# Other instruction orders at the end of a memory stage and in the last stage of a four-layer kernel

## The chip, the cores and the metric

The kernel runs on one core of one Trainium2 chip. The metric is the device time of one execution in microseconds (us), the median of three runs.

## The reference

Four blocks follow one another on 4096 tokens of width 256, each with a residual and a layer normalization: gated linear attention, a mixture of experts, a neural memory, and an MLP with ternary weights. The change touches the end of the third and all of the fourth. Cut to what matters:

```python
# third block (memory): a two-layer residual MLP (W1, W2) is trained for one step on all tokens
keys, queries, values = x @ Wk + bk, x @ Wq + bq, x @ Wv + bv
grads = grad of sum(mean((lmm(params, keys) - values)**2) * alr)
params = p * (1 - LR * WD) - LR * g / (sqrt(g * g) + EPS)
x = layernorm(x + lmm(new_params, queries))      # h = h + silu(h @ W + b), twice
# fourth block
h = relu(x @ Wq1.T + b1)                          # Wq1, Wq2: weights rounded to -1, 0, 1
x = layernorm(x + h @ Wq2.T + b2)
```

## The kernel before

The tokens are cut into eight blocks of 512 (`NB = 8`), called tiles here. X holds the tokens by rows, XT by columns. Each engine has its own hand-written list of instructions, and semaphores order them among the engines; nothing is planned at run time, so an instruction that waits holds up everything behind it on its engine. A product of a 512-token tile with a 256x256 weight (`plane`, line 1230) writes a pair of PSUM banks and shows as 8 matmul records.

**The memory stage** (`build_memory`, line 1238) makes the gradients. PSUM has a ring of three bank pairs there, and `pair(q, use)` picks a pair from the tile's number and one of 11 uses in fixed rotation; two more banks collect the gradients of W1 and W2. For the last tile, q = 7, TensorE (PE) does the second layer, `grad1` of tile 6, the turns of h0 and h1 (transposes that ScalarE, ACT, copies out), then `back` (W2T times dz2), the turn of dz2, `grad2`, the turn of dz1 and `grad1`. Among these stand five products `queries(0)` to `queries(4)` (query projections of tiles 0 to 4, which the next stage needs; ACT evicts each with its bias into XT, line 1582). VectorE (DVE) makes dz2 (line 1718) and dz1 (1732), and at the end the optimizer step of W2 after `g2_ready` and of W1 after `g1_ready` (lines 1803 to 1807). The stage ends when all engines have ended their lists.

**The last stage** (`build_read_and_mlp`, line 1833) reads the memory with the new weights and applies the MLP. An iteration q handles three tiles at once: of tile q `first` (banks RA), `second` (banks RB) and `turn_h`; of tile q - 1 `normalize` on ACT (line 2100) and `turn_x`, `x_hi`, `x_lo`; of tile t = q - 2 the MLP: eight `up(t, f)` (line 1948, 4 matmul records, one bank each, `bH[f % 2]`), ACT's two evictions `hidden(t, f)` (lines 2094 and 2095), the subtraction on GpSimd (POOL, line 2298) and eight `down(t, f)` (line 1958, 8 records, sums over f in the banks bO). `up(t, f)` waits until ACT has read its bank for f - 2; `down(t, f)` waits for POOL's `hl_done`. `down(t, 6)` and `down(t, 7)` slip into the next iteration, ahead of its `up`s. After the last `down`, DVE adds the result (`add_out`, line 2195); `down(t, 0)` waits for the `add_out` of tile t - 1 (`out_done`). `finish(q - 4, ..)` on ACT (line 2107) is the last normalization of a tile, from scales that DVE computes (`scales`, lines 2314 to 2320 and 2236). Iteration q = 2 has its own list on PE, `third`; the last two tiles are done by `drain`, with four banks for `up`; DVE ends with `last_half(0)` and `last_half(1)` (lines 2246 to 2263).

DVE's order in a middle iteration is: `first` (lines 2162 and 2171, the h1 add), `add_out`, its statistics, `add_b2` (2201), `x_lo` (2207), `second`, the residual, statistics, `scales`.

Of the kernel before, what the change touches and what calls it, by code (L numbers as in the profile page):

```python
# [1226 lines left out]
NB = NTOK // 512  # L1227
# [10 lines left out]
def build_memory(nc, io, mem):  # L1238

    X, XT, ident, slot = mem["X"], mem["XT"], mem["ident"], mem["slot"]  # L1240
    with ExitStack() as c2:
# [52 lines left out]
        td2_ready, td2_read, td1_ready, td1_read = sem("td2_ready"), sem("td2_read"), sem("td1_ready"), sem("td1_read")  # L1294
# [13 lines left out]
        def pair(q, use):  # L1308

            return ring[(11 * q + use) % 3]  # L1310

        with nc.Block() as block:
            @block.sync
            def _(sp):
# [26 lines left out]
            def _(pe):  # L1341
# [45 lines left out]
                def back(q):  # L1387
                    if q + 1 < NB:
                        pe.wait_ge(k_read, 2 * (q + 2))
                    else:  # L1390
                        pe.wait_ge(q_read, 2)
                    pe.wait_ge(dz2_done, 2 * (q + 1))
                    plane(pe, pair(q, DH), W2T, lambda i: dz2[:, i, :]).then_inc(dh_ready, 1)

# [10 lines left out]
                def turn_h1(q):  # L1405
                    pe.wait_ge(sl2_done, 2 * (q + 1))
                    turn(pair(q, TH1), h1).then_inc(th1_ready, 1)

                def turn_dz2(q):
                    if q + 1 < NB:  # L1410
                        pe.wait_ge(v_read, 2 * (q + 2))
                    else:
                        pe.wait_ge(q_read, 4)
                    turn(pair(q, TD2), dz2).then_inc(td2_ready, 1)

                def turn_dz1(q):
                    pe.wait_ge(dz1_done, 2 * (q + 1))
                    turn(pair(q, TD1), dz1).then_inc(td1_ready, 1)
# [8 lines left out]
                def grad1(q):  # L1427
                    pe.wait_ge(th0_read, 2 * (q + 1))
                    pe.wait_ge(td1_read, 2 * (q + 1))
                    grad(0, "h0", "dz1").then_inc(g1_ready, 1)  # L1430
# [6 lines left out]
                def queries(j, b):  # L1437
                    plane(pe, b, Wq, tokens(j)).then_inc(q_ready, 1)
# [8 lines left out]
                q = NB - 1  # L1447
# [44 lines left out]
                grad1(q - 1)  # L1492
                turn_h0(q)
                turn_h1(q)
                pe.wait_ge(th0_read, 2 * NB)
                queries(0, pair(q, KEY))
                pe.wait_ge(td1_read, 2 * (NB - 1))
                queries(1, pair(q, VAL))
                back(q)
                turn_dz2(q)  # L1500
                pe.wait_ge(th1_read, 2 * NB)
                queries(2, pair(q, Z1))
                grad2(q)
                pe.wait_ge(dh_done, 2 * (q + 1))
                turn_dz1(q)
                grad1(q)
                pe.wait_ge(td2_read, 2 * NB)
                queries(3, pair(q + 1, Z2))
                pe.wait_ge(q_read, 2 * 3)
                queries(4, pair(q + 1, TH0))  # L1510

            @block.scalar
            def _(act):
# [65 lines left out]
                def queries(j, b):  # L1579
                    act.wait_ge(q_ready, j + 1)  # L1580
                    for g in range(G):
                        act.activation(XT[:, g, j * 512:(j + 1) * 512], b[g][:, :], ACT.Identity, bias=bq[:, g:g + 1]).then_inc(q_read, 1)
# [35 lines left out]
                second(q)  # L1618
                keep_h0(q)
                keep_h1(q)  # L1620
                queries(0, pair(q, KEY))
                queries(1, pair(q, VAL))
                keep_dz2(q)
                queries(2, pair(q, Z1))
                keep_dz1(q)
                queries(3, pair(q + 1, Z2))
                queries(4, pair(q + 1, TH0))

            @block.vector
            def _(v):  # L1630
# [202 lines left out]
def build_read_and_mlp(nc, io, mem, out):  # L1833
# [4 lines left out]
    with ExitStack() as c2:  # L1838
# [31 lines left out]
        def block_of(q):  # L1870
            return 0 <= q < NB
# [4 lines left out]
        with nc.Block() as block:  # L1876
# [18 lines left out]
            def _(pe):  # L1895
# [7 lines left out]
                def second(q):  # L1903
                    if q >= 1:
                        pe.wait_ge(res_done, 2 * q)
                    pe.wait_ge(h1_done, 2 * (q + 1))
                    plane(pe, RB, W2n, lambda i: h1[:, i, :]).then_inc(z2_ready, 1)
# [44 lines left out]
                def down(q, f):  # L1952
                    pe.wait_ge(hl_done, FC * q + f + 1)
                    if f == 0 and q >= 1:
                        pe.wait_ge(out_done, 2 * q)
                    for k in range(4):
                        for part in range(2):
                            mm = pe.matmul(bO[k // 2][:, (k % 2) * D:(k % 2 + 1) * D], hr[:, part, f, k * P:(k + 1) * P], W2r[:, f, :],  # L1958
                                           start=(f == 0 and part == 0 and k % 2 == 0), stop=(f == FC - 1 and part == 1), skip_group_check=True)
                        if f == FC - 1 and k % 2 == 1:  # L1960
                            mm.then_inc(o_ready, 1)
# [13 lines left out]
                def third():  # L1975
                    first(2)
                    turn_h(1)
                    for f in range(4):
                        up(0, f)
                    down(0, 0)  # L1980
                    second(2)
                    down(0, 1)
                    turn_x(1)
                    down(0, 2)
                    up(0, 4)
                    down(0, 3)
                    up(0, 5)
                    turn_h(2)
                    down(0, 4)
                    up(0, 6)  # L1990
                    down(0, 5)
                    up(0, 7)
# [28 lines left out]
                for q in range(NB):  # L2021
                    t = q - 2
                    if q == 2:
                        third()
                        continue
                    if block_of(q):
                        first(q)
                    if q == 0:
                        queries(5, bH)
                    if q == 1:  # L2030
                        pe.wait_ge(q_read, 2)
                        queries(7, bH)
                    if block_of(q - 3):
                        down(q - 3, 6)
                        down(q - 3, 7)
                    if block_of(t):
                        up(t, 0)
                        up(t, 1)
                        up(t, 2)
                        up(t, 3)  # L2040
                        down(t, 0)
                        down(t, 1)
                    if block_of(q - 1):
                        turn_x(q - 1)
                    if block_of(q):
                        second(q)
                    if q == 0:
                        queries(6, bO)
                    if block_of(t):
                        down(t, 2)  # L2050
                        up(t, 4)
                        down(t, 3)
                        up(t, 5)
                    if q != 1:
                        turn_h(q)
                    if block_of(t):
                        down(t, 4)
                        up(t, 6)
                        down(t, 5)
                        up(t, 7)  # L2060
# [3 lines left out]
            def _(act):  # L2064
# [52 lines left out]
                for q in range(NB + 3):  # L2117
                    t = q - 2
                    if block_of(q):
                        first(q)  # L2120
                    if q == 0:
                        act.wait_ge(wq_in, 32)
                        queries(5, 0, bH)
                    if block_of(q - 4):
                        finish(q - 4, 0, 2)
                    if block_of(t):
                        if t == 0:
                            act.wait_ge(b_in, 32)
                        hidden(t, 0)
                        hidden(t, 1)  # L2130
                    if block_of(q - 1) and q != 2:
                        normalize(q - 1)
                    if q == 1:
                        queries(7, 2, bH)
                    if block_of(t):
                        hidden(t, 2)
                        hidden(t, 3)
                    if q == 2:
                        normalize(1)
                        second(2)  # L2140
                    if block_of(q - 1):
                        x_hi(q - 1)
                    if block_of(q) and q != 2:
                        second(q)
                    if q == 0:
                        queries(6, 1, bO)
                    if block_of(t):
                        for f in range(4, FC):
                            hidden(t, f)
                    if block_of(q - 4):  # L2150
                        finish(q - 4, 2, 4)
# [276 lines left out]
```

## Time and profile before

| | us |
|---|---|
| median of three runs | 1381.18 |
| lowest and highest | 1378.48 and 1381.18 |
| the profiled execution | 1380.95 |
| its span (first to last instruction) | 1379.2 |
| PE busy in the span | 1312.8 (95%) |
| DVE, ACT, POOL busy | 803.0, 573.7, 300.9 |

The profiled execution is one run with the hardware profiler; its time is its span and 1.75 us around it. In a timeline a row is a run of like instructions: start, length, engine, line, operation, what is written from what, count, and in brackets how long the engine was idle before and what released it. Two lengths may overlap, since an instruction starts before the one ahead has fully drained; the distance between starts is the pace.

### The profile page before, as it was taken

The numbers are of one execution on the slowest core, as the hardware profiler recorded it, in microseconds if no ns is written. First come the engines' busy times: TensorE is split into PE (matmuls) and PEld (weight loads), VectorE is DVE, ScalarE is ACT, GpSimd is POOL, SyncE is SP. The second block draws the span as 40 slices with busy tenths as digits, with TensorE's granted clock in tenths as the row PEclk, the third lists the DMA queues.
The fourth block names the chain that finished last, engine by engine and source line by source line (L and its number), as shares of the span: only waits on it lengthen the run. The fifth ranks groups of instructions, "written<-read, shape, count | busy, mean of one in ns | idle before, by whom it ended". The sixth has DMA issues, their size and how long they took to land. (4 is left out here: it accounts for less than half of the span.)

```text
span 1379.2 us, 22623 instructions
## 1 busy us (share of the span) xinstructions
PE 1312.8 (95%) x7786; PEld 831.0 (60%) x7788; DVE 803.0 (58%) x1558; ACT 573.7 (42%) x1256; POOL 300.9 (22%) x345
## 2 busy tenths in 40 slices
PE   8899999899998999999999999889999999999997
PEld 4556666645555666666666665446665564577776
DVE  6999999965541222222222222477778755776777
ACT  5667777551110222222222221334343532566676
POOL 1133333314760000000000000732220000234444
PEclk9999999999999999999999999999999999999999
DMA  7666665666220111111111111423110000000001
GB/s 233 213 211 215 213 209 192 219 227 215 93 97 15 39 46 46 46 46 46 43 45 43 44 46 42 142 66 103 39 39 8 8 8 12 1 1 16 16 31 62
DMA packets 78342, 118.47 MB, mean 86 GB/s; under 512 B 9489, under 2 KB 63025, under 8 KB 74289
## 3 DMA queue, kind: packets, MB, share of 16 engines
q1 hardware_dynamic: 71696, 100.52, 22.1%
q0 software_dynamic: 6144, 16.79, 3.8%
q8 instruction: 53, 0.87, 0.3%
q14 instruction: 33, 0.26, 0.1%
q10 hardware_dynamic: 416, 0.03, 0.0%
HBM read 84.98 MB, written 32.33 MB: 85 GB/s over the span
## 5 line engine op out<-in xcount | busy, mean ns | idle before, releaser
L1824 POOL DMA_INDIRECT m_got<-outs,slot x64 | 62.7, 980 | 543.1 <-DMA outs<-XT 450.6
L1209 DVE TENSOR_TENSOR ro_h<-ro_bB,ro_sl 128x512 f32<-128x512 f32 x71 | 49.1, 692 | 217.2 <-PE ro_bB L1158 217.2
L2298 POOL TENSOR_TENSOR q_hr<-q_hf,q_hr 128x512 fp32r<-128x512 f32 x64 | 84.0, 1324 | 264.8 <-ACT q_hr L2095 264.8
L625 DVE TENSOR_TENSOR_SCAN a_dcy<-a_gbc,a_ident 128x2048 f32<-128x2048 f32 x31 | 137.7, 4443 | 3.9
L1165 PEld LDWEIGHTS ro_bO<-Wout,ro_hT 128*128 128x128 f32 x568 | 107.9, 190 | 45.6 <-issue 34.6
L1153 PE MATMUL ro_bA<-Win,ro_xT 128*128 x284 | 134.6, 596 | 0.7 <-ACT ro_xT L1180 0.6
L1165 PE MATMUL ro_bO<-Wout,ro_hT 128*128 x568 | 134.3, 379 | 0.9 <-DVE ro_hT L1202 0.9
L1158 PE MATMUL ro_bB<-Wsw,ro_xT 128*128 x284 | 133.5, 592 | 0.0
L1189 ACT ACTIVATE XT<-ro_bO 128x256 f32<-128x256 f32 x71 | 27.2, 383 | 204.9 <-PE ro_bO L1165 204.9
L1202 DVE COPY ro_hT<-ro_bH 128x512 f32<-128x512 f32 x71 | 49.1, 692 | 101.2 <-PE ro_bH L1138 101.2
L1158 PEld LDWEIGHTS ro_bB<-Wsw,ro_xT 128*128 128x128 f32 x284 | 54.0, 190 | 67.9 <-issue 67.9
L1184 ACT ACTIVATE ro_sl<-ro_bA 128x512 f32<-128x512 f32 x71 | 42.4, 597 | 96.0 <-PE ro_bA L1153 96.0
L1054 POOL DMA_INDIRECT rows<-r_row,r_rix x64 | 63.6, 994 | 53.7 <-DVE r_rix L955 35.8
L642 DVE TENSOR_TENSOR a_A<-a_bS,a_dcy 128x1024 f32<-128x1024 f32 x64 | 75.1, 1215 | 0.1
L721 POOL TENSOR_TENSOR a_qk<-a_eb,a_rb 128x512 f32<-128x512 f32 x28 | 36.6, 1308 | 160.7 <-ACT a_eb L470 160.7
L1153 PEld LDWEIGHTS ro_bA<-Win,ro_xT 128*128 128x128 f32 x284 | 48.3, 190 | 35.5 <-issue 35.1
L1958 PE MATMUL q_bO<-W2r,q_hr 128*128 128x256 f32 x448 | 66.2, 294 | 1.4 <-POOL q_hr L2298 1.4
L1958 PEld LDWEIGHTS q_bO<-W2r,q_hr 128*128 128x128 f32 x448 | 58.0, 188 | 12.1 <-POOL q_hr L2298 6.5
L1234 PE MATMUL m_ring<-m_h,m_W 128*128 128x512 f32 x128 | 60.6, 618 | 4.6 <-DVE m_h L1674 3.5
L1948 PE MATMUL q_bH<-q_xr,W1r 128*128 128x512 f32 x224 | 61.3, 402 | 2.6 <-ACT q_hr L2095 2.6
L906 ACT ACTIVATE sh_sl<-sh_bA 128x512 f32<-128x512 f32 x28 | 16.7, 596 | 112.1 <-PE sh_bA L836 104.5
L1423 PE MATMUL m_gW<-m_t_dz,m_t_h 128*128 128x256 f32 x256 | 57.9, 379 | 1.3 <-ACT m_t_dz L1561 1.3
(302 smaller groups left out, 2484.4 us busy)
## 6 DMA issues: line engine op xcount, KB each, us to landing
a_gbc<-gd SPq DMA_DIRECT2D x31, 1024.0 KB, 5.1
rows<-a_zero SPq DMA_DIRECT2D x8, 1152.0 KB, 9.4
XT<-rows SPq DMA_DIRECT2D x71, 128.0 KB, 2.0
outs<-XT SPq DMA_DIRECT2D x71, 128.0 KB, 1.7
a_xt<-in_xTt SPq DMA_DIRECT2D x8, 512.0 KB, 5.8
X<-in_x SPq DMA_DIRECT2D x8, 512.0 KB, 4.0
Win<-in_w_in SPq DMA_DIRECT2D x8, 512.0 KB, 10.3
Wsw<-in_w_sw SPq DMA_DIRECT2D x8, 512.0 KB, 10.1
```

What stands on the lines that cost most here:

```text
L625: v.tensor_tensor_scan(dcy[:, :], gbc[j % 2][:, :], ident16[:, :], 0.0, ALU.mult, ALU.add).then_inc(d_done, 1)
L642: v.tensor_tensor(A[j % 2][:, 2 * h:2 * h + 2, :, :, :].rearrange("p r g e t -> p r g (e t)"), bS[:, 2 * h:2 * h + 2, :].rearrange("p r (g ...
L1054: pool.indirect_dma_start(out=mem["rows"], out_offset=bass.IndirectOffsetOnAxis(ap=rix[p][k][:, 0:1], axis=0), in_=row[p][k][:, :], in_off ...
L1153: mm = pe.matmul(bA[:, :], xT[p][:, g, :], w, start=(g == 0), stop=(g == G - 1))
L1158: mm = pe.matmul(bB[:, :], xT[p][:, g, :], w, start=(g == 0), stop=(g == G - 1))
L1165: mm = pe.matmul(bO[:, 0:D], hT[:, j * P:(j + 1) * P], Wout[:, bass.ds(e, 1), j, :].rearrange("p o f -> p (o f)"), start=(j == 0), stop=(j ...
L1234: mm = pe.matmul(banks[o][:, :], W[:, i, col + o * P:col + (o + 1) * P], rhs(i), start=(i == 0), stop=(i == G - 1))
L1423: mm = pe.matmul(gW[k][:, i * D:(i + 1) * D], tok[left][:, t, i * P:(i + 1) * P], tok[right][:, t, :], start=False, stop=False, skip_group ...
L1824: pool.indirect_dma_start(out=got[q % 2][k][:, t, :], out_offset=None, in_=mem["outs"], in_offset=bass.IndirectOffsetOnAxis(ap=slot[:, k, ...
L1948: mm = pe.matmul(hidden_bank(q, f)[:, :], W1r[:, g, f * P:(f + 1) * P], xr[q % 2][:, part, g, :], start=(g == 0 and part == 0), stop=(g == ...
L1958: mm = pe.matmul(bO[k // 2][:, (k % 2) * D:(k % 2 + 1) * D], hr[:, part, f, k * P:(k + 1) * P], W2r[:, f, :], start=(f == 0 and part == 0 ...
L2298: pool.tensor_tensor(hr[:, 1, f, :], hf[f % 2][:, :], hr[:, 0, f, :], ALU.subtract).then_inc(hl_done, 1)
```

## The change

Four edits of order; no instruction is added or removed, and no arithmetic changes.

- Memory stage, PE and ACT: the five query products stand at other places and use other bank pairs. `queries(0)` takes the pair VAL and no longer waits for `th0_read`; `back` follows it and no longer waits for a query eviction; `queries(2)` stands between the turn of dz1 and `grad1`.
- Last stage, PE, `third`: `down(0, 1)` goes ahead of `second(2)`.
- Last stage, PE, iterations 3 to 7: `down(t - 1, 6)` and `down(t - 1, 7)` go behind `up(t, 0)` and `up(t, 1)`, as `drain` already has it for tile 6.
- Last stage, ACT, iterations 8 to 10: `finish(q - 4, 0, 2)` goes behind `hidden(t, 0)` and `hidden(t, 1)`.

```diff
--- before.py
+++ after.py
@@ -1309,6 +1309,8 @@
 
             return ring[(11 * q + use) % 3]
 
+        last_bank = [pair(NB - 1, use) for use in (VAL, TH1, TD2, Z1, TD1)]
+
         with nc.Block() as block:
             @block.sync
             def _(sp):
@@ -1387,8 +1389,6 @@
                 def back(q):
                     if q + 1 < NB:
                         pe.wait_ge(k_read, 2 * (q + 2))
-                    else:
-                        pe.wait_ge(q_read, 2)
                     pe.wait_ge(dz2_done, 2 * (q + 1))
                     plane(pe, pair(q, DH), W2T, lambda i: dz2[:, i, :]).then_inc(dh_ready, 1)
 
@@ -1410,7 +1410,7 @@
                     if q + 1 < NB:
                         pe.wait_ge(v_read, 2 * (q + 2))
                     else:
-                        pe.wait_ge(q_read, 4)
+                        pe.wait_ge(q_read, 2)
                     turn(pair(q, TD2), dz2).then_inc(td2_ready, 1)
 
                 def turn_dz1(q):
@@ -1492,22 +1492,23 @@
                 grad1(q - 1)
                 turn_h0(q)
                 turn_h1(q)
+                pe.wait_ge(td1_read, 2 * (NB - 1))
+                queries(0, last_bank[0])
                 pe.wait_ge(th0_read, 2 * NB)
-                queries(0, pair(q, KEY))
-                pe.wait_ge(td1_read, 2 * (NB - 1))
-                queries(1, pair(q, VAL))
                 back(q)
                 turn_dz2(q)
                 pe.wait_ge(th1_read, 2 * NB)
-                queries(2, pair(q, Z1))
+                queries(1, last_bank[1])
                 grad2(q)
                 pe.wait_ge(dh_done, 2 * (q + 1))
                 turn_dz1(q)
+                pe.wait_ge(td2_read, 2 * NB)
+                queries(2, last_bank[2])
                 grad1(q)
-                pe.wait_ge(td2_read, 2 * NB)
-                queries(3, pair(q + 1, Z2))
-                pe.wait_ge(q_read, 2 * 3)
-                queries(4, pair(q + 1, TH0))
+                pe.wait_ge(q_read, 2 * 2)
+                queries(3, last_bank[3])
+                pe.wait_ge(td1_read, 2 * NB)
+                queries(4, last_bank[4])
 
             @block.scalar
             def _(act):
@@ -1618,13 +1619,12 @@
                 second(q)
                 keep_h0(q)
                 keep_h1(q)
-                queries(0, pair(q, KEY))
-                queries(1, pair(q, VAL))
+                queries(0, last_bank[0])
                 keep_dz2(q)
-                queries(2, pair(q, Z1))
+                queries(1, last_bank[1])
                 keep_dz1(q)
-                queries(3, pair(q + 1, Z2))
-                queries(4, pair(q + 1, TH0))
+                for j in range(2, 5):
+                    queries(j, last_bank[j])
 
             @block.vector
             def _(v):
@@ -1978,8 +1978,8 @@
                     for f in range(4):
                         up(0, f)
                     down(0, 0)
+                    down(0, 1)
                     second(2)
-                    down(0, 1)
                     turn_x(1)
                     down(0, 2)
                     up(0, 4)
@@ -2030,12 +2030,11 @@
                     if q == 1:
                         pe.wait_ge(q_read, 2)
                         queries(7, bH)
-                    if block_of(q - 3):
-                        down(q - 3, 6)
-                        down(q - 3, 7)
                     if block_of(t):
                         up(t, 0)
+                        down(t - 1, 6)
                         up(t, 1)
+                        down(t - 1, 7)
                         up(t, 2)
                         up(t, 3)
                         down(t, 0)
@@ -2121,13 +2120,15 @@
                     if q == 0:
                         act.wait_ge(wq_in, 32)
                         queries(5, 0, bH)
-                    if block_of(q - 4):
+                    if block_of(q - 4) and q < NB:
                         finish(q - 4, 0, 2)
                     if block_of(t):
                         if t == 0:
                             act.wait_ge(b_in, 32)
                         hidden(t, 0)
                         hidden(t, 1)
+                    if q >= NB:
+                        finish(q - 4, 0, 2)
                     if block_of(q - 1) and q != 2:
                         normalize(q - 1)
                     if q == 1:
```

## Rows read from the trace of the kernel before

**Rows 1.** The page's busy time, share of the span and instructions of each engine

```profile
PE 1312.8 (95%) x7786; PEld 831.0 (60%) x7788; DVE 803.0 (58%) x1558; ACT 573.7 (42%) x1256; POOL 300.9 (22%) x345
```

**Rows 2.** Timeline, PE, end of the memory stage (start us, us, what, idle before, releaser)

```profile
1119.47 1.91 PE L1398 MATMUL m_ring<-ident,m_h 128*128 128x128 f32 x16
1121.68 7.13 PE L1234 MATMUL m_ring<-XT,m_Wq 128*128 128x512 f32 x16 [0.30 <-ACT m_t_h L1561]
...
1132.96 3.60 PE L1234 MATMUL m_ring<-XT,m_Wq 128*128 128x512 f32 x8
...
1139.85 1.04 PE L1398 MATMUL m_ring<-ident,m_dz 128*128 128x128 f32 x8
1142.15 3.69 PE L1423 MATMUL m_gW<-m_t_dz,m_t_h 128*128 128x256 f32 x16 [1.27 <-ACT m_t_dz L1561]
1145.68 7.03 PE L1234 MATMUL m_ring<-XT,m_Wq 128*128 128x512 f32 x16
1154.32 3.67 PE L1234 MATMUL q_RA<-XT,W1n 128*128 128x512 f32 x8 [1.61 <-PEq L1312]
```

**Rows 3.** Timeline, DVE, end of the memory stage

```profile
1124.35 0.09 DVE L1718 DVE_READ_ACCUMULATOR2_ANT m_btmp<- 128x1 f32 x1
...
1140.12 0.69 DVE L1803 TENSOR_SCALAR m_ga<-m_gW 128x512 f32<-128x512 f32 x1 [4.12 <-PE m_gW L1423]
...
1151.96 0.69 DVE L1807 SCALAR_TENSOR_TENSOR W1n<-m_W,m_ga 128x512 f32<-128x512 f32 x1
```

**Rows 4.** Timeline, PE, then ACT, third tile of the last stage (q = 2)

```profile
1193.13 3.67 PE L1234 MATMUL q_RB<-q_h,W2n 128*128 128x512 f32 x8 [1.65 <-DVE q_h L2171]
...
1197.59 1.52 PE L1930 MATMUL q_RA<-ident,X 128*128 128x128 f32 x8
...
1196.54 2.08 ACT L2100 ACTIVATE X<-X,q_shift,q_rstd 128x256 f32<-128x256 f32 x4 [4.43 <-DVE q_shift L2236]
```

**Rows 5.** Timeline, PE, one middle tile (q = 4)

```profile
1235.47 2.46 PE L1958 MATMUL q_bO<-W2r,q_hr 128*128 128x256 f32 x16
1237.77 2.03 PE L1948 MATMUL q_bH<-q_xr,W1r 128*128 128x512 f32 x8
1240.22 2.36 PE L1948 MATMUL q_bH<-q_xr,W1r 128*128 128x512 f32 x8 [0.42 <-ACT q_hr L2095]
1242.42 2.06 PE L1958 MATMUL q_bO<-W2r,q_hr 128*128 128x256 f32 x16
```

**Rows 6.** Timeline, ACT, then DVE, the same tile

```profile
1237.23 1.08 ACT L2107 ACTIVATE X<-X,q_shift,q_rstd 128x256 f32<-128x256 f32 x2
1238.91 0.69 ACT L2094 ACTIVATE q_hf<-q_bH,q_b 128x512 f32<-128x512 f32 x1 [0.59 <-PE q_bH L1948]
...
1238.20 1.28 DVE L2171 TENSOR_TENSOR q_h<-XT,q_sl 128x512 f32<-128x512 f32 x2
1239.40 1.28 DVE L2195 TENSOR_TENSOR X<-q_bO,X 128x512 f32<-128x512 f32 x2
...
1246.10 1.29 DVE L2207 TENSOR_TENSOR q_xr<-q_RA,q_xr 128x512 fp32r<-128x512 f32 x2 [2.22 <-ACT q_xr L2087]
```

**Rows 7.** Timeline, DVE in tile q = 2, then POOL in tile q = 3

```profile
1189.79 3.19 DVE L2171 TENSOR_TENSOR q_h<-XT,q_sl 128x512 f32<-128x512 f32 x2
...
1215.39 2.54 POOL L2298 TENSOR_TENSOR q_hr<-q_hf,q_hr 128x512 fp32r<-128x512 f32 x2 [4.97 <-ACT q_hr L2095]
```

**Rows 8.** Timeline, PE, then ACT, first part of the drain

```profile
1339.14 1.21 PE L1958 MATMUL q_bO<-W2r,q_hr 128*128 128x256 f32 x8 [1.39 <-POOL q_hr L2298]
1340.18 1.17 PE L1930 MATMUL q_RA<-ident,X 128*128 128x128 f32 x8
...
1335.50 1.10 ACT L2107 ACTIVATE X<-X,q_shift,q_rstd 128x256 f32<-128x256 f32 x2 [1.25 <-DVE q_shift L2236]
...
1338.78 2.08 ACT L2100 ACTIVATE X<-X,q_shift,q_rstd 128x256 f32<-128x256 f32 x4
```

**Rows 9.** Timeline, DVE, the last half tile

```profile
1371.61 0.69 DVE L2246 TENSOR_TENSOR X<-q_bO,X 128x512 f32<-128x512 f32 x1 [0.17 <-PE q_bO L1970]
```

## The prediction

> **What bounds the kernel now.** I read the page first: PE is busy 95% of the span, no other engine over 58% [rows 1]. So time can only come from PE's idle gaps, and an order that leaves a gap where it was gains nothing. Then I took PE's timeline through the stretches that the diff touches and read the brackets: how long PE waited, and for whom. At the memory stage's end it waits 0.30 us for the turned h0, 1.27 us for the turned dz1, and 1.61 us for ACT's last eviction and the change of stage [rows 2]. In the third tile of the last stage it waits 1.65 us for DVE's h1 add [rows 4]. Each of the five middle tiles (q = 3 to 7) has the same gap at its third `up`, 0.42 us by the bracket [rows 5]. In the drain it waits 1.39 us for POOL [rows 8]. For each gap the other engines' timelines say what would be late next.
>
> **Memory stage.** Same work, other order, so I lay it out anew from 1119.47. Paces come from starts: 16 transposes 1.74 (8 are 0.87), a product 3.43, a gradient 3.46; the last two sum to 1139.85 - 1132.96 = 6.89 [rows 2]. `queries(0)` no longer waits: 1121.21 instead of 1121.68. It ends at 1124.64; dz2 is ready at 1124.44 [rows 3], so `back` follows at once, to 1128.07. Turn of dz2 to 1128.94, `queries(1)` to 1132.37, `grad2` to 1135.83, turn of dz1 to 1136.70, `queries(2)` to 1140.13, `grad1` to 1143.59. The 1.27 us wait for ACT's copy of dz1 is covered by `queries(2)`, three times as long. `queries(3)` and `(4)` start at 1143.59 instead of 1145.68 [rows 2], a gain of 2.09. The remaining waits (ACT's evictions of about 1.3 us) each lie behind a product of 3.43. Is DVE late next? Its two optimizer steps take 12.53 us from `grad2`'s end [rows 3]; `grad2` now ends near 1136.0, so W2 is done at 1142.3, W1 waits for `grad1` (1143.8) and ends near 1150.1. PE's last product ends at 1150.6, and ACT's eviction follows. The 1.61 us at the stage change stays [rows 2]. **Term: -2.05 us**, bounds -1.6 (only the two brackets' 1.57) and -2.1.
>
> **`down(0, 1)` ahead of `second(2)`.** It fills 0.95 of the 1.65 us gap. But the `turn_x(1)` behind takes 1.52 us where eight transposes take 1.04: it waits for ACT's normalization, which starts at 1196.54 after waiting 4.43 us for DVE's scales and lasts 2.08 [rows 4]. That chain (h1 add, scales, normalization) runs through DVE and ACT and is not shortened, so `turn_x(1)` ends as before. **Term: 0**, bounds 0 and -0.3.
>
> **Middle tiles.** In tile q = 4, `first` ends at 1237.77 - 1.88 = 1235.89, two `down`s being 1.88 ahead of the `up` [rows 5]. Before: `up` 0 and 1 are done at 1239.65, the third `up` starts at 1240.22, and the first `down` at 1242.42 where without waits it would be at 1241.53: 0.89 lost. The cause is that two banks serve four `up`s, and ACT's eviction of the first runs from 1238.91 [rows 6] until PE goes on at 1240.22. New order: `up` 0 to 1236.83, `down` 6 to 1237.77, `up` 1 to 1238.71, `down` 7 to 1239.65. ACT is busy with `finish` from 1237.23; the next ACT instruction follows 1.00 behind, as in the drain (1335.50 to 1336.50, its 1.10 less 0.1 of overlap) [rows 6, 8]. The evictions then start at 1238.23 instead of 1238.91 [rows 6], 0.68 earlier, and free the first bank at 1239.54 (PE started 1.31 after them). The third `up` starts at 1239.65 unhindered; the fourth and the `down` behind it hang on the second bank, and so come 0.7 earlier: 1241.7 instead of 1242.42. 0.7 saved, and ACT, not PE, sets it. The products' last half now ends 1.88 later, at about 1239.8. DVE reaches `add_out` at 1239.40 [rows 6] and ends it at 1240.7, before `down` needs it at 1241.7. The normalization on ACT starts 0.7 earlier, so `turn_x` is not held.
>
> Tile q = 3 has no `finish`, so POOL's subtraction (1215.39 [rows 7]) starts some 1.6 us earlier, on top of the h1 adds, which in tile 4 begin 2.3 us behind `first` [rows 5, 6]. What that costs the row of tile q = 2 shows: two h1 adds under POOL's subtractions took 3.19 us instead of 1.28 [rows 6, 7]. Here one add would wait a subtraction, about 1.2 us; `add_out` then ends 0.4 us after `down(1, 0)` could start, and tile 3 saves 0.5. Without such waits tile 3 would save its full 0.9, and the sum below would be 0.4 larger. The Trainium skill states the exclusion as a rule in SBUF — State Buffer, "Who interferes with whom": a DVE instruction with two SBUF inputs and a GpSimd instruction that reads SBUF block each other for a whole instruction, by issue order. By that rule, the trace agrees. **Term: -(4 x 0.7 + 0.5) = -3.3 us**, bounds -4.5 (five full 0.9) and -2.0 (0.4 per tile).
>
> **Drain.** ACT starts `finish(4)` at 1335.50, after 1.25 us of waiting for DVE's scales, and PE waits 1.39 us behind it [rows 8]. With the two `hidden` ahead, ACT does them in the time it used to wait: from about 1334.15 to 1336.4 (its list was free at 1334.25). `finish` takes 0.98, and normalization of tile 7 starts at 1337.4 instead of 1338.78 [rows 8]: 1.38 earlier, although it stands later in the order. The first `down` starts 1.5 earlier; `turn_x(7)`, bound by that normalization, 1.4 earlier, and everything behind follows it. **Term: -1.4 us**, bounds 0 and -1.6. In the last tile the move starts POOL's chain of eight subtractions up to 1 us earlier, but DVE's scales of tile 6 exclude it in turns, and DVE's last half waits for PE only 0.17 us [rows 9]: that is all PE can still win there. **Term: -0.1 us**, bounds +1.3 (one subtraction more in the chain, half of the 2.54 us pair [rows 7]) and -0.2.
>
> **Sum:** -2.05 - 0 - 3.3 - 1.4 - 0.1 = -6.85, from the profiled 1380.95 to 1374.1. The median is 0.23 above that run, within what this sum can tell, and I keep 1374.1; one of three runs lay 2.7 below the median. About 0.2%, 2.8 us, is what a measurement can tell.
>
> **Rivals.**
> - *The exclusion eats the middle tiles.* Tiles 4 to 7 have 0.08 us between the end of the h1 add (1239.48 [rows 6]) and POOL's new start, about 1239.56. If the second add falls behind a subtraction there, `add_out` ends at about 1242.0 and a tile saves 0.4: the middle term is -2.0, the sum -5.55, the time 1375.4. For it: the margin is smaller than any jitter. Against it: the order of the two is fixed by ACT's list, and the margin is positive. Chance 0.15.
> - *The tail turns out otherwise.* DVE and POOL alternate there; one subtraction more on the chain costs 1.4 against the -0.1: 1375.5. If ACT's and DVE's chains also keep the drain where it was, +1.4: 1376.9. Chance 0.13.
> - *The moves do not do what they say.* The gap moves from the third `up` to the fourth or to `down` in the middle tiles, and the memory stage saves only a part: -0.5 there and -1.4 in the drain, 1379. For it: in tile q = 2 that is what I expect. Against it: ACT is idle 0.59 us before the eviction in question [rows 6]. Chance 0.05.
> - *Slower.* `add_out` waits for the last product, 1.88 us later now, and DVE works in order: the statistics, `x_lo` and the second layer's adds stand behind it, and with these `turn_h`. If DVE had no slack, each middle tile would be 1.88 longer: 1380.95 + 5 x 1.88 - 2.05 - 1.4 = 1386.9. It decides once DVE is late by more than its idle time before `x_lo`, 2.22 us [rows 6]. By the rows it is late by 0.1 to 0.4. Chance 0.03.
>
> **Numbers.** The forecast has 0.64. The range takes in the first two rivals, the terms' bounds and the runs' 2.7 us downward: 1371.0 to 1377.0. Faster by over 0.2%: 0.64 + 0.15 + 0.13 and a little of the third, 0.93; within 0.2%: 0.04; slower: 0.03.
>
> **What would show it.** In the profile of the changed kernel: no wait at `queries(0)` and at `grad1` of tile 7, the stage change near 1152.2; PE's gap before `second(2)` down to 0.7 and `turn_x(1)` as late as before; in tiles 4 to 7 the third `up` without a wait, the fourth with a little one, and a period 0.7 shorter, with `add_out` still right behind the h1 add; in tile 3 one h1 add lengthened from 0.68 to about 1.9; in the drain the first `down` without the 1.39 us wait and ACT at work while DVE makes its scales. The prediction is wrong if the middle tiles' period stays, if `turn_x(1)` comes earlier, or if POOL's chain in the last tile moves the end by more than 0.5 us either way.

## The result and the profile after

The changed kernel took 1372.91 us, the median of six runs (1371.38 to 1376.07), against 1380.83 us (1378.48 to 1381.18) before: ratio 0.9944, 95% interval 0.9934 to 0.9954. It is faster by 7.9 us in the medians. The forecast was 1374.1 us. Its profiled execution took 1376.07 us, with a span of 1374.3, only 4.9 us below the span before. The reason is not in the change: the turns of the last tile's h0 and h1, where the first edited stretch begins, start at 1121.80 instead of 1119.47 [rows 2], 2.33 us later in code that is the same. So I compare stretches between fixed instructions, not totals.

The page's busy times: PE is still busy 95%, in a shorter span.

```profile
PE 1308.5 (95%) x7786; PEld 830.1 (60%) x7788; DVE 803.6 (58%) x1558; ACT 572.8 (42%) x1256; POOL 301.6 (22%) x345
```

**Memory stage.** PE's timeline of the changed kernel, to be laid beside [rows 2]:

```profile
1121.80 1.91 PE L1398 MATMUL m_ring<-ident,m_h 128*128 128x128 f32 x16
1123.55 3.60 PE L1234 MATMUL m_ring<-XT,m_Wq 128*128 128x512 f32 x8
...
1139.05 3.60 PE L1234 MATMUL m_ring<-XT,m_Wq 128*128 128x512 f32 x8
1142.49 3.62 PE L1423 MATMUL m_gW<-m_t_dz,m_t_h 128*128 128x256 f32 x16
1145.94 7.03 PE L1234 MATMUL m_ring<-XT,m_Wq 128*128 128x512 f32 x16
1154.58 3.67 PE L1234 MATMUL q_RA<-XT,W1n 128*128 128x512 f32 x8 [1.61 <-PEq L1314]
```

The waits of 0.30 and 1.27 us are gone, and every start follows the one ahead at the pace of its kind. From the turns to the last stage's first product it is 32.78 us instead of 34.85: -2.07. DVE, to be laid beside [rows 3]:

```profile
1146.21 0.69 DVE L1803 TENSOR_SCALAR m_ga<-m_gW 128x512 f32<-128x512 f32 x1 [1.51 <-PE m_gW L1423]
...
1151.77 0.69 DVE L1807 SCALAR_TENSOR_TENSOR W1n<-m_W,m_ga 128x512 f32<-128x512 f32 x1
```

The second optimizer step now waits 1.51 us for `grad1`, and ends at 1152.46, 0.5 us before PE's last product (1152.97) and 1.8 before ACT's last eviction (1154.27). DVE is not late, but near.

**Third tile.** PE, then ACT, as [rows 4]:

```profile
1193.41 3.67 PE L1234 MATMUL q_RB<-q_h,W2n 128*128 128x512 f32 x8 [0.72 <-DVE q_h L2172]
1197.56 1.82 PE L1930 MATMUL q_RA<-ident,X 128*128 128x128 f32 x8 [0.48 <-ACT X L2099]
...
1196.82 2.08 ACT L2099 ACTIVATE X<-X,q_shift,q_rstd 128x256 f32<-128x256 f32 x4 [4.45 <-DVE q_shift L2237]
```

PE's wait before `second(2)` fell from 1.65 to 0.72 us, and a new one of 0.48 stands before the turn of x, which is also longer (1.82 for 1.52), because it waits for ACT piece by piece. Tile 3 starts 53.28 us behind the stage's first product, as before. The gap has moved.

**Middle tiles.** PE, then ACT, then DVE in tile q = 4, as [rows 5, 6]:

```profile
1235.32 1.50 PE L1948 MATMUL q_bH<-q_xr,W1r 128*128 128x512 f32 x4
1236.66 1.11 PE L1958 MATMUL q_bO<-W2r,q_hr 128*128 128x256 f32 x8
1237.61 1.09 PE L1948 MATMUL q_bH<-q_xr,W1r 128*128 128x512 f32 x4
1238.55 1.11 PE L1958 MATMUL q_bO<-W2r,q_hr 128*128 128x256 f32 x8
1239.50 2.22 PE L1948 MATMUL q_bH<-q_xr,W1r 128*128 128x512 f32 x8
1241.55 2.04 PE L1958 MATMUL q_bO<-W2r,q_hr 128*128 128x256 f32 x16
...
1237.07 1.08 ACT L2106 ACTIVATE X<-X,q_shift,q_rstd 128x256 f32<-128x256 f32 x2
1238.06 0.68 ACT L2093 ACTIVATE q_hf<-q_bH,q_b 128x512 f32<-128x512 f32 x1
...
1238.04 1.28 DVE L2172 TENSOR_TENSOR q_h<-XT,q_sl 128x512 f32<-128x512 f32 x2
1239.24 1.28 DVE L2196 TENSOR_TENSOR X<-q_bO,X 128x512 f32<-128x512 f32 x2
```

`up` and `down` alternate 0.94 us apart. The two last `up`s take 2.22 us, not 2.03: the fourth waits a little for its bank. ACT's evictions start 0.99 behind `finish`, with no wait between. DVE's `add_out` follows the h1 adds at once. In tile q = 3 it is otherwise (PE, DVE, POOL):

```profile
1217.35 2.12 PE L1958 MATMUL q_bO<-W2r,q_hr 128*128 128x256 f32 x16 [0.24 <-DVE X L2196]
...
1213.63 2.38 DVE L2172 TENSOR_TENSOR q_h<-XT,q_sl 128x512 f32<-128x512 f32 x2
...
1214.00 1.46 POOL L2299 TENSOR_TENSOR q_hr<-q_hf,q_hr 128x512 fp32r<-128x512 f32 x1 [3.33 <-ACT q_hr L2094]
```

POOL's subtraction starts 0.37 us into the two h1 adds; these take 2.38 instead of 1.28 us (the first 0.67, the second 1.78), the subtraction 1.46 instead of 1.28, and PE's first `down` waits 0.24 us for DVE's `add_out`.

**Drain and tail.** PE, then ACT, then DVE, as [rows 8]:

```profile
1334.57 1.12 PE L1958 MATMUL q_bO<-W2r,q_hr 128*128 128x256 f32 x8
1335.52 1.44 PE L1930 MATMUL q_RA<-ident,X 128*128 128x128 f32 x8
...
1331.11 0.68 ACT L2093 ACTIVATE q_hf<-q_bH,q_b 128x512 f32<-128x512 f32 x1
...
1333.39 1.10 ACT L2106 ACTIVATE X<-X,q_shift,q_rstd 128x256 f32<-128x256 f32 x2
1334.38 2.09 ACT L2099 ACTIVATE X<-X,q_shift,q_rstd 128x256 f32<-128x256 f32 x4
...
1332.27 0.17 DVE L2237 SCALAR_TENSOR_TENSOR q_shift<-q_mv,q_rstd 128x8 f32<-128x8 f32 x1
```

ACT does the two evictions while DVE still makes the scales (ready at 1332.44), and `finish` starts without a wait. The first `down` has none either. The last rows of PE and DVE, as [rows 9]:

```profile
1360.53 4.54 PE L1970 MATMUL q_bO<-W2r,q_hr 128*128 128x256 f32 x36 [0.50 <-POOL q_hr L2299]
...
1361.90 0.16 DVE L2237 SCALAR_TENSOR_TENSOR q_shift<-q_mv,q_rstd 128x4 f32<-128x4 f32 x1
...
1366.74 0.69 DVE L2247 TENSOR_TENSOR X<-q_bO,X 128x512 f32<-128x512 f32 x1
```

The last half tile on DVE no longer waits for PE, which was done at 1365.07. The scales of tile 6 end 25.10 us behind the end of `turn_x(7)`, where they ended 25.34 behind it. DVE from `add_b2` of the last tile on, in the kernel before (three rows), then in the changed one:

```profile
1357.61 1.32 DVE L2201 TENSOR_TENSOR X<-X,q_b 128x1024 f32<-128x1024 f32 x1
...
1364.28 1.23 DVE L2318 TENSOR_TENSOR q_na<-q_rstd 128x4 f32<-128x4 f32 x1
...
1366.53 0.16 DVE L2236 SCALAR_TENSOR_TENSOR q_shift<-q_mv,q_rstd 128x4 f32<-128x4 f32 x1
...
1353.22 2.16 DVE L2202 TENSOR_TENSOR X<-X,q_b 128x1024 f32<-128x1024 f32 x1
...
1359.28 1.21 DVE L2320 SCALAR_TENSOR_TENSOR q_na<-q_na,q_nt 128x4 f32<-128x4 f32 x1
```

`add_b2` takes 0.84 us more, but of the tiny operations behind it (0.16 us each where POOL is idle) only four take 1.2 us beside a subtraction of POOL, where it was five: POOL's last subtraction ends 0.63 us earlier behind `turn_x(7)`.

The stretches, as distances between starts of PE (and the span's end), in us:

| stretch | before | after | difference | predicted |
|---|---|---|---|---|
| turns of the last tile to the last stage | 34.85 | 32.78 | -2.07 | -2.05 |
| last stage to `first(3)` | 53.28 | 53.28 | 0 | 0 |
| tile 3 | 24.84 | 24.42 | -0.42 | -0.5 |
| tiles 4, 5, 6 | 24.85, 24.83, 24.84 | 24.10, 24.12, 24.13 | -2.17 | -2.1 |
| tile 7, to `up(5, 7)` | 23.91 | 23.20 | -0.71 | -0.7 |
| from there to the end of `turn_x(7)` | 10.48 | 9.12 | -1.36 | -1.4 |
| from there to the end | 37.83 | 37.34 | -0.49 | -0.1 |
| sum | | | -7.22 | -6.85 |

### The profile page after: what moved, and what is told of

It is laid out like the page before. It is cut to its first block and busy times, and to the rows that moved or that the text cites. A ratio compares the mean times of both kernels' runs of the same rounds, so it can differ in the third digit from the quotient of the medians.

```text
span 1374.3 us, 22623 instructions
## 1 busy us (share of the span) xinstructions
PE 1308.5 (95%) x7786; PEld 830.1 (60%) x7788; DVE 803.6 (58%) x1558; ACT 572.8 (42%) x1256; POOL 301.6 (22%) x345
```

## The experiments

The four parts and the last two kernels ran on two chips where the kernel before took 1381 us, the other six on two where it took 1412. There the stages ahead of the edits were slower: the memory stage's first key product started 38.0 to 38.2 instead of 28.0 us behind the experts' last product, for one. Stretches with the same order took the same on all of them to 0.05 us, with one exception (53.38 us for 53.28 in the stage's first three tiles, in `only_mid`), and they are what I compare.

### Each part alone

`only_mem`, `only_third`, `only_mid` and `only_fin` are the kernel before with one part of the diff each. `only_mem` has the hunks of the diff up to line 1627 (`last_bank`, `back`, `turn_dz2` and the two lists of the memory stage); the others:

```diff
 # only_third
                     down(0, 0)
+                    down(0, 1)
                     second(2)
-                    down(0, 1)
 # only_mid
-                    if block_of(q - 3):
-                        down(q - 3, 6)
-                        down(q - 3, 7)
                     if block_of(t):
                         up(t, 0)
+                        down(t - 1, 6)
                         up(t, 1)
+                        down(t - 1, 7)
 # only_fin
-                    if block_of(q - 4):
+                    if block_of(q - 4) and q < NB:
                         finish(q - 4, 0, 2)
...
+                    if q >= NB:
+                        finish(q - 4, 0, 2)
```

> The kernel before with the memory stage's part of the change alone. Theory (two waits of PE covered, nothing else late): the stretch from the turns of the last tile's h0 and h1 to the last stage's first product is 2.07 us shorter than in the kernel before (34.85 to 32.78), the last stage keeps its length, total -2.1 us. Rival (the next stage takes it back, for instance because its weights are not loaded yet): the last stage grows by as much, total within 0.5 us.

> The kernel before with down(0, 1) ahead of second(2) alone. Theory (the turn of x waits for DVE's scales and ACT's normalization): PE's wait before second(2) falls from 1.65 to 0.72 us, one of about 0.5 us appears before turn_x(1), the first product of tile 3 starts as late as before behind the stage's first product (53.28 us), total 0. Rival (the wait is simply filled): -0.9 us.

> The kernel before with the interleaved ups and downs of iterations 3 to 7 alone. Theory (ACT's finish sets tiles 4 to 7, the exclusion of DVE and POOL sets tile 3): tile 3 0.42 us shorter, tiles 4 to 7 0.7 each, total -3.3 us; the drain from then on as in the kernel before. Rival (the drain and the tail depend on the phase of DVE against POOL, which moves): another 1 us either way behind tile 7.

> The kernel before with finish(q - 4, 0, 2) behind the two hidden in iterations 8 to 10 alone. Theory (ACT works while it used to wait for DVE's scales): the wait of 1.39 us before the drain's first down is gone, everything behind the turn of tile 7 is 1.4 us earlier, and the tail gains 0 to 0.5 more: total -1.4 to -1.9 us. Rival (the gain needs the earlier parts): less than 0.5 us.

| | ratio to before, 95% interval | memory stage | tiles 3 to 6 | to end of `turn_x(7)` | to the span's end |
|---|---|---|---|---|---|
| before | 1 | 34.85 | 24.84, 24.85, 24.83, 24.84 | 34.39 | 72.22 |
| only_mem | 0.9982, 0.9973 to 0.9991 | 32.78 | 24.84, 24.84, 24.86, 24.84 | 34.38 | 71.98 |
| only_third | 1.0002, 0.9992 to 1.0012 | 34.85 | 24.87, 24.84, 24.83, 24.83 | 34.39 | 72.28 |
| only_mid | 0.9975, 0.9966 to 0.9984 | 34.85 | 24.40, 24.12, 24.12, 24.12 | 33.67 | 71.54 |
| only_fin | 0.9992, 0.9983 to 1.0001 | 34.85 | 24.81, 24.86, 24.84, 24.85 | 33.01 | 70.37 |

(The last two columns count from the start of `first(7)`.) Each part changes its own stretch by what the whole change does there and leaves the others alone: -2.07 us for `only_mem`, 0 for `only_third`, -0.44 and four times -0.72 for `only_mid`, -1.38 for `only_fin`. Up to the end of `turn_x(7)` the parts add. The theories of the first three hold and their rivals fall: nothing is taken back behind the memory stage; `only_third` moves PE's wait (0.72 before `second`, 0.49 before the turn) and no more; nothing of 1 us happens behind tile 7. `only_fin` gains 1.85 us in the stretches, 0.47 of it in the tail, as expected. Its total alone would not show it: the interval of the ratio just reaches 1.

`only_mem` also shows something that the edit can't cause: the end is 0.24 us nearer with the same instructions in the same order. PE's last products, first of the kernel before, then of `only_mem`:

```profile
1365.55 6.03 PE L1970 MATMUL q_bO<-W2r,q_hr 128*128 128x256 f32 x36 [0.71 <-POOL q_hr L2298]
...
1364.19 4.49 PE L1970 MATMUL q_bO<-W2r,q_hr 128*128 128x256 f32 x36 [0.71 <-POOL q_hr L2298]
```

Both are the same 36 records. Stretches of 5 us of the kernel before, then the same stretches of `only_mem`, which is 1.36 us ahead there (length, busy time and count of PE, PEld, DVE, ACT, POOL, granted clock, DMA share, GB/s):

```profile
1360.00:1365.00 5.00, 3.72 (x21) 2.84 (x20) 4.79 (x7) 4.64 (x8) 4.63 (x5) 1.00 0.01 2
1365.00:1370.00 5.00, 4.45 (x24) 4.45 (x25) 4.02 (x18) 2.19 (x5) 0.49 (x1) 0.66 0.37 125
...
1358.64:1363.64 5.00, 3.72 (x21) 2.84 (x20) 4.79 (x7) 4.64 (x8) 4.63 (x5) 1.00 0.00 2
1363.64:1368.64 5.00, 4.45 (x36) 4.29 (x36) 4.01 (x18) 2.20 (x5) 0.49 (x1) 1.00 0.37 124
```

The granted clock fell to 1.2 GHz in part of the last products in one run (0.66 on average) and stayed at 2.4 GHz in the other (1.00), after the same work: PE 3.72 us busy of 5 in both, in the same 21 products with short waits between. At the lower clock the products take 1.5 us more, but the end comes only 0.24 later, since DVE itself could start its last half no more than that before PE was done.

So in the tail the parts don't simply add. `down_first` (below) has `finish` behind the `hidden`s and the lower clock in the last products. PE, then DVE:

```profile
1391.00 6.03 PE L1970 MATMUL q_bO<-W2r,q_hr 128*128 128x256 f32 x36 [0.51 <-POOL q_hr L2299]
...
1397.20 0.69 DVE L2247 TENSOR_TENSOR X<-q_bO,X 128x512 f32<-128x512 f32 x1
```

PE is done at 1397.03, DVE starts at 1397.20 without waiting, and from `turn_x(7)` to the end it is 37.35 us, as in the changed kernel (37.34). With `finish` where it was, it is 37.83 to 37.89 at the lower clock (three traces) and 37.60 without it. So the edit is worth 0.5 us where the clock falls (one trace) and 0.25 where it doesn't.

### What covers the copy of dz1

```diff
 # q2_late, against the changed kernel (PE)
-                pe.wait_ge(td2_read, 2 * NB)
-                queries(2, last_bank[2])
                 grad1(q)
+                pe.wait_ge(td2_read, 2 * NB)
+                queries(2, last_bank[2])
```

> The changed kernel with queries(2) behind grad1 of the last tile instead of ahead of it. Theory (queries(2) covers ACT's copy of dz1): PE waits 1.27 us before grad1 again, and the stretch from the turns to the last stage is 32.78 + 1.5 = 34.3 us. Rival (the gain comes from the new banks and the early queries(0) alone): no wait there, 32.8 us.

PE in front of `grad1`:

```profile
1167.09 3.69 PE L1423 MATMUL m_gW<-m_t_dz,m_t_h 128*128 128x256 f32 x16 [1.27 <-ACT m_t_dz L1562]
```

The wait of 1.27 us is back, and the stretch takes 34.28 us, 1.50 more. The place of `queries(2)` is worth 1.5 of the 2.07 us. The other 0.57 is gained ahead of it, 0.47 of it at the start of `queries(0)`; the free banks that allow this were not tried by themselves.

### The order within the pairs

```diff
 # down_first, against the changed kernel (PE, iterations 3 to 7)
-                        up(t, 0)
                         down(t - 1, 6)
-                        up(t, 1)
+                        up(t, 0)
                         down(t - 1, 7)
+                        up(t, 1)
                         up(t, 2)
```

> The changed kernel with each pair turned round in iterations 3 to 7: down 6, up 0, down 7, up 1. Theory (what counts is how early each up is issued, against ACT's evictions): up 0 is 0.94 us later than in the changed kernel, which ACT's finish still hides, up 1 0.94 later, so the second bank is freed about 0.5 later; tiles 4 to 7 are 0.4 to 0.6 us longer than in the changed kernel (24.5 to 24.7), still shorter than 24.84. Rival (any interleaving does): 24.12 us as in the changed kernel.

PE in a tile of it (`up` 1 and 2, then the fourth):

```profile
1267.07 2.03 PE L1948 MATMUL q_bH<-q_xr,W1r 128*128 128x512 f32 x8
1269.52 1.20 PE L1948 MATMUL q_bH<-q_xr,W1r 128*128 128x512 f32 x4 [0.42 <-ACT q_hr L2094]
```

The fourth `up` waits 0.42 us for its bank; tiles 3 to 6 take 24.61, 24.62, 24.61 and 24.60 us, as expected (24.5 to 24.7). Against 24.84 before, this order saves 0.23 us; the other 0.49 comes from issuing the `up`s one `down` earlier. That it is the second of them that counts was part of the expectation and was not tried by itself.

### ACT's finish in the middle tiles

```diff
 # finish_late, against the changed kernel (ACT)
-                    if block_of(q - 4) and q < NB:
-                        finish(q - 4, 0, 2)
                     if block_of(t):
...
                         hidden(t, 1)
-                    if q >= NB:
+                    if block_of(q - 4):
                         finish(q - 4, 0, 2)
```

> The changed kernel with finish(q - 4, 0, 2) behind the two hidden in all iterations, so in 4 to 7 as well. Theory (ACT's finish held the evictions, but it also kept POOL off the h1 adds of DVE): POOL's subtraction starts under the h1 adds, which take about 2.3 us instead of 1.28 as in tile 3, add_out is late, and tiles 4 to 7 take 24.4 us like tile 3 instead of 24.12; total +1.2 us against the changed kernel. Rival (only ACT's place matters): 23.95 us per tile, total -0.7 us.

DVE, then POOL, then PE in tile 4 of this kernel:

```profile
1268.52 2.38 DVE L2170 TENSOR_TENSOR q_h<-XT,q_sl 128x512 f32<-128x512 f32 x2
...
1268.90 1.46 POOL L2297 TENSOR_TENSOR q_hr<-q_hf,q_hr 128x512 fp32r<-128x512 f32 x1 [3.29 <-ACT q_hr L2094]
...
1272.25 2.12 PE L1958 MATMUL q_bO<-W2r,q_hr 128*128 128x256 f32 x16 [0.24 <-DVE X L2194]
```

The same picture as tile 3 of the changed kernel, to the hundredth: adds of 2.38 us, a subtraction of 1.46, and PE waiting 0.24 us for `add_out`. Tiles 4 to 6 take 24.38, 24.38 and 24.44 instead of 24.10 to 24.13. The rival, that only ACT's place matters, falls: `finish` holds ACT's evictions, and that keeps POOL off DVE. What is best in the drain is worse in the middle tiles. (Totals can't tell: `finish_late` has a ratio to the kernel before of 0.9957, 0.9938 to 0.9975, and the next kernel, `norm_split`, 0.9955, 0.9939 to 0.9971.)

### The same cover for tile 3

```diff
 # norm_split, against the changed kernel (ACT)
                     if block_of(q - 4) and q < NB:
                         finish(q - 4, 0, 2)
+                    if q == 3:
+                        normalize(2, 0, 2)
...
                         hidden(t, 1)
...
-                    if block_of(q - 1) and q != 2:
+                    if q == 3:
+                        normalize(2, 2, 4)
+                    elif block_of(q - 1) and q != 2:
                         normalize(q - 1)
```

(`normalize` takes the range of its four parts here.)

> The changed kernel with the first two of the four normalizations of tile 2 ahead of the two hidden in iteration 3, where finish stands in the later ones. Theory (tile 3 lost to the exclusion of POOL and DVE): POOL starts 1 us later, behind the h1 adds, these take 1.28 instead of 2.38 us, and tile 3 takes 24.12 instead of 24.42 us: -0.3 us. Rival (the h1 adds are slow for another reason, or ACT's two operations cost as much as they save): 24.4 us or more.

DVE, then POOL in tile 3:

```profile
1241.49 1.28 DVE L2176 TENSOR_TENSOR q_h<-XT,q_sl 128x512 f32<-128x512 f32 x2
...
1242.84 2.55 POOL L2303 TENSOR_TENSOR q_hr<-q_hf,q_hr 128x512 fp32r<-128x512 f32 x2 [4.30 <-ACT q_hr L2094]
```

POOL starts 0.07 us behind the h1 adds, these take 1.28 us, and the tile takes 24.15 instead of 24.42: -0.27. Starting later is faster here. POOL need not even wait for the end of the adds: in tile 3 of `down_first` it starts 0.20 us before it, the adds take 1.28 us as well, and the first subtraction 1.36.

### The tail

```diff
 # b2_early, against the changed kernel (DVE)
+                    if q == NB + 1:
+                        add_b2(q - 2)
                     if block_of(q - 3):
                         add_out(q - 3)
...
-                    if block_of(q - 2):
+                    if block_of(q - 2) and q <= NB:
                         add_b2(q - 2)
```

> The changed kernel with DVE's add_b2 of the last tile ahead of add_out of tile 6, in DVE's idle 4 us, instead of behind its statistics. Theory (the tail's end is set by DVE's chain add_out, add_b2, scales of tile 6, last_half(0), last_half(1), drawn out by turns with POOL): the scales of tile 6 end 0.8 to 1.5 us earlier, last_half(1) starts when PE is done, about 0.7 to 1.2 us earlier; total -0.7 to -1.2 us. Rival (POOL's chain of subtractions sets the end through PE): less than 0.3 us.

The stretch from `first(7)` to the end takes 68.77 instead of 69.66 us: -0.89, within what was expected. The scales of tile 6 end 0.88 earlier too, and POOL's last subtraction 0.49 earlier. One part of the theory failed: `last_half(1)` doesn't start when PE is done (1392.77) but 1.33 us later, at 1394.10, so DVE's own list still sets the end. Its ratio to the kernel before was 0.9941 (0.9916 to 0.9966) on one of the slower chips.

`both` has `b2_early` and `norm_split` together.

> The changed kernel with both additions: add_b2 of the last tile early, and the normalization of tile 2 split. Theory: the gains add, -1.0 to -1.5 us against the changed kernel, about 1371.7 where that measures 1372.9. Rival (the phase of DVE against POOL in the tail changes with the shift): the sum is off by one POOL subtraction, 1.3 us.

In the stretches the gains add: tile 3 24.17, the last stretch 68.84 us. Its total was 1406.23 us (ratio 0.9972, 0.9948 to 0.9996), worse than `b2_early`'s 1403.58; on that chip the kernel before ran from 1405.19 to 1421.39, and a us can't be told. So it ran again beside the changed kernel, on one of the faster chips:

> The changed kernel once more, beside the one with both additions. Theory: each stretch as in its first trace (32.78 us at the memory stage's end, tile 3 24.42, tiles 4 to 7 24.12, 69.7 us from the last tile's first product to the end), since these depend on the order alone, while the total differs with what comes before. Rival (the stretches vary too): off by more than 0.2 us.

> The changed kernel with add_b2 of the last tile early and the normalization of tile 2 split. Theory: by the stretches 0.27 + 0.85 = 1.1 us less than the changed kernel on the same chip, ratio 0.9992. Rival (totals are not the sum of the stretches): the same as the changed kernel or slower.

| | median, range | ratio to before, 95% interval | tile 3 | `first(7)` to the end |
|---|---|---|---|---|
| after_again | 1374.67 (1373.64 to 1378.34) | 0.9948, 0.9935 to 0.9962 | 24.38 | 69.66 |
| both_again | 1372.63 (1371.42 to 1372.85) | 0.9932, 0.9918 to 0.9945 | 24.14 | 68.82 |

All stretches of `after_again` are those of the changed kernel's first trace to 0.05 us, so the rival, that they vary too, falls.

DVE in the last iterations of `both_again`: `add_b2` now lies in what was idle time, ahead of `add_out`, and the scales end at 1358.82.

```profile
1343.70 1.22 DVE L2206 TENSOR_TENSOR X<-X,q_b 128x1024 f32<-128x1024 f32 x1
1347.79 1.29 DVE L2200 TENSOR_TENSOR X<-q_bO,X 128x512 f32<-128x512 f32 x2 [2.88 <-PE q_bO L1958]
...
1358.66 0.16 DVE L2241 SCALAR_TENSOR_TENSOR q_shift<-q_mv,q_rstd 128x4 f32<-128x4 f32 x1
```

The stretches say -1.1 us against the changed kernel, on two chips; the totals differ by 2.0 us with ranges that do not meet, part of which is variation ahead of the edits (the profiled runs reach the last tile's turns at 1124.07 and 1119.62 us). So this kernel is faster than the changed one by about 1.1 us in its stretches, less than totals alone can show: the intervals of the two ratios overlap.

## Why the prediction was right

The forecast was 1374.1 us in a range of 1371.0 to 1377.0, and 1372.91 was measured. The terms are compared in the stretches:

- **Memory stage, -2.05.** Measured -2.07 in all nine traces that have the whole edit (32.78 or 32.79 us). Less the 2.33 us of offset, each start came out within 0.03 us of the one laid out. That `queries(2)` covers the copy of dz1 is shown by `q2_late`. Nothing is late next: DVE ends 0.5 us before PE's last product, as forecast.
- **`down(0, 1)`, 0.** The stretch is 53.28 us before and after, and 53.30 in `only_third`. The wait moved to the turn of x, as the chain through scales and normalization said.
- **Middle tiles, -3.3.** Measured -3.3. The forecast had ACT, not PE, set tiles 4 to 7, and the exclusion of DVE and POOL set tile 3. `finish_late` and `norm_split` show both: with POOL's start moved 1 us either way the loss of 0.3 us goes where the overlap goes. The margin that the first rival doubted, 0.08 us, is 0.07 in the trace (h1 adds to 1239.32, POOL from 1239.39), and 0.06 to 0.08 in every trace with the new order and `finish` in front. In tile 3 the second h1 add takes 1.78 us, forecast was 1.9. That tile 3 would save 0.9 without the exclusion is not shown: `norm_split` takes the exclusion away and delays ACT in the same step, and saves 0.69.
- **Drain, -1.4.** Measured -1.36. The normalization of tile 7 stands later in ACT's order and starts earlier in time.
- **Tail, -0.1, bounds +1.3 and -0.2.** Measured -0.49: outside its bounds, and the one step that failed. I had reasoned that PE could only win the 0.17 us that DVE waited for it. In its place: the scales of tile 6 on DVE end 0.24 us earlier than the shift explains, since one of its tiny operations fewer stands beside a subtraction of POOL, which saves more than the 0.84 us that `add_b2` loses. The other 0.25 us is the wait for PE in the kernel before: its last products ran in part at 1.2 GHz, and DVE could have started 0.25 us earlier (0.17 in the bracket, and the overlap with the operation ahead). `only_mem` loses that wait by the clock alone, without any edit there; `down_first` loses it at the lower clock by the edit, since POOL and so PE's last products are 0.6 us ahead. The turns I had considered, and bounded too tightly; the clock I had not looked at in that stretch. The end moved by 0.49 us, just short of the 0.5 that the prediction had named as a sign of being wrong.
- **The rivals.** The exclusion eating tiles 4 to 7 does happen, but only in `finish_late`. (With the 0.5 of tile 3 that rival's middle term is -2.1, not -2.0.) `add_out` was late in tile 3 alone, by 0.24 us at PE, far from the 2.22 us at which the slower case would have begun.

The stretches sum to -7.22 us. The ratio's interval allows 6.4 to 9.1 us, and the difference of the medians is 7.9; the rest is no more than the variation ahead of the edits, where the traces of the two faster chips differ by 5.4 us (1118.70 to 1124.07 at the last tile's turns).

## What to carry to other kernels

When one engine is busy 95%, walk its timeline for the waits in brackets, and for each ask which chain frees the next instruction: a gap filled in front of a chain that stays just moves (third tile), one filled with work that lets the chain start earlier is gained (the `up`s, `queries(2)`). Compare small changes by stretches between fixed instructions: here they repeated to 0.05 us, once to 0.1, where totals varied by 5 and more. And an operation on ACT that looks like a delay can be what keeps GpSimd and VectorE from overlapping; ahead of moving it, look whether an add of VectorE with both inputs in SBUF lies beside it.

## What the runs showed of the hardware

- Two VectorE adds with both inputs in SBUF and two subtractions on GpSimd, with GpSimd starting 0.37 us into the adds, cost 1.10 us on VectorE (2.38 for 1.28) and 0.2 each on GpSimd (1.46 and 1.50 for 1.28), the same in both kernels where it happened. With GpSimd starting 0.07 us behind the adds it costs nothing, and starting 0.20 us before their end (tile 3 of `down_first`) it costs nothing on VectorE and 0.08 on GpSimd (1.36). The Trainium skill, SBUF — State Buffer, "Who interferes with whom", states the mutual blocking by issue order; by that rule, the trace agrees.
- Operations of VectorE on 128x4 elements, 0.16 us each where GpSimd is idle, took 1.2 us where they fell beside GpSimd's subtractions at the end of the last stage: five of them in the kernel before, four in the changed one.
- The last 36 records of PE took 6.04, 6.06 and 6.03 us in `only_third`, `only_mid` and `down_first`, as in the kernel before (6.03, where the granted clock fell to 1.2 GHz), and 4.49 to 4.55 in the other ten traces, `only_mem` (4.49) and the changed kernel (4.54) among them. The kernel before and `only_mem` have the same order there and stand on both sides, and so do `down_first` and the changed kernel, so the order alone does not decide it, and what does stays open.
- Ahead of the edits, the same instruction (the last tile's turns) was reached at 1118.70 to 1124.07 us on the two faster chips, at 1119.62 and 1124.07 on one of them, and at 1147.79 to 1152.26 us on the two slower ones. A difference of 2 us in single spans says nothing of an edit.
